# Division of a layer-1 attention stage among GpSimd, VectorE and DMA, and its order by half beats, in one fused two-layer kernel

## The chip, the core and the metric

One core of one Trainium2 chip. The metric is the device time of one launch in microseconds (us); lower is better. PE is TensorE's matmul, PEld its weight load, DVE is VectorE, ACT is ScalarE, POOL is GpSimd, SP is SyncE, which here only issues DMAs.

## The reference, cut to what matters

The whole program is two transformer-like layers over 2048 tokens (4 batches of 512) of 512 channels. The change touches only the last stage, layer 1:

```
xn = layernorm(x);  q = xn @ Wq.T                    # 32 heads of 16 channels
q, k = rmsnorm(q), rmsnorm(k)                        # per head
o  = softmax(q k^T / 4) v                            # keys and values of ctx_2048
x3 = x + tanh(g) * o
# spline layer, per token:
xf = layernorm(x3)*gamma + beta
tile = argmax over 64 tiles of sign scores (first the best of 8 clusters)
s  = the 8 channels of xf that belong to that tile
mn, mx = min and max of s over all tokens that chose the same tile
out = x3 + tanh(g2) * (xf, with those 8 channels replaced by a spline of (s-mn)/(mx-mn))
```

So attention needs the queries of a whole batch, and the very last result (the spline) needs the minimum and maximum over all tokens.

## The kernel before, in words

`phase_back` (from L1420) does this stage in one block, with one straight-line instruction list per engine. Time is counted in half beats `h` from -18 to 80. Each engine runs `for h in range(START, END)` and calls, in a written order, the steps whose slot plus lag equals `h`; each engine takes its list strictly in order and waits on semaphores. There are three kinds of work:

- **Groups of heads** (`g_at`): 32 groups, eight for each batch, group n from half beat 2n. PE computes scores (`scores`, L1643), ACT the exponentials (`exps`, L1818, 8 per group), PE multiplies by the values (`weigh`, L1655) into one of two PSUM tiles `atpO`. At lag 2 DVE copies that tile out (`evacuate`, L1862), PE transposes it (`turn`, L1662), and at lag 3 DVE divides by the sums (`normalise`, L1868 and L1869, into `o`). `weigh` of group n waits for `normalise` of group n-2, since both use the same PSUM tile.
- **Query tiles** (`q_at` with `q_slot`, `n_at` with `n_slot`): 16 tiles of 128 tokens. The first four (FIRST) come before group 0. Of each later tile: SP loads `x2a` and `x1` (`load`, L1555 and L1556, lag -2); POOL adds them (`combine`, L1716, lag 0); DVE takes mean and variance (`spread`, L1874, lag 1), POOL the root (`root`, L1721), DVE normalises and casts to f16 (`norm`, L1883 and L1887, lag 2), POOL subtracts for the low half (`low`, L1725, lag 2), SP turns the tile with a transposing DMA (`turn`, L1561, lag 3), PE projects it (`project`, L1678, twelve matmuls, six at the end of one group and six in the next), DVE copies the result (`projected`, L1892, lag 6), POOL squares it (`square`, L1730), DVE sums (`squares`, L1901), for each pair of tiles takes the root by Newton steps (`roots`, L1910 to L1915), scales (`scale`, L1923), POOL casts (`high`, L1735), DVE subtracts (`parts`, L1929), SP stores to `qst` (`store`, L1565), and SP reads queries back by a transposing DMA (`queries`, lag -3) for each group.
- **Spline tiles** (`c_at` with `c_slot`): 16 tiles of 128 tokens, when the groups of their batch are done. POOL adds `o` to `x2` (`residual`, L1740, lag 0); DVE `spread2` (L1948 to L1954, lag 1), POOL `roots` (L1744), DVE `scales` (L1959 to L1961, lag 2), POOL `y` (L1748), ACT `signs` (L1823), DVE `choose` (L1967 to L1975, lag 4), POOL `gathers` (two indirect DMAs, L1752 and L1755, lag 5), DVE `inner` (L1980 to L1992, lag 6). After the last `inner` come a short chain on PE and DVE and 16 indirect scatters on POOL (L1782).

In each half beat DVE's written order is: `projected`, `evacuate`, `inner`, `choose`, `normalise`, `scales`, `parts`, `scale`, `squares` with `roots`, `spread2`, `norm`, `spread`. POOL's is: `gathers`, `residual`, `combine`, `low`, `root`, `roots`, `high`, `square`, `y`. Slots before:

```python
q_slot = [-16, -15, -14, -13, -4, -2, 0, 2] + [16 * b + 6 + 4 * j for b in range(2) for j in range(4)]
c_slot = [16 * b + 19 + 4 * j for b in range(3) for j in range(4)] + [65, 66, 67, 68]
n_slot = {i: q_slot[i] + 7 for i in range(5, NT, 2)}
```

Of the kernel before, what the change touches and what calls it, by code (L numbers as in the profile page):

```python
# [15 lines left out]
P = 128  # L16
# [296 lines left out]
def part_pair(ap, first, step):  # L313

    return bass.AP(ap.tensor, ap.offset + first * HD, [list(ap.ap[0]), [4 * HD, NH], [step * HD, 2], [1, HD]])

# [1113 lines left out]
def phase_back(nc, S, sb, ps, a, R, K, out, wq):  # L1430
# [15 lines left out]
    with ExitStack() as mem:  # L1446
# [5 lines left out]
        xin = [sb(mem, f"quxin{i}", [P, D]) for i in range(4)]  # L1452
# [29 lines left out]
        key = [sb(mem, f"lakey{i}", [P, NTILE]) for i in range(2)]  # L1482
        top = [sb(mem, f"latop{i}", [P, 8]) for i in range(2)]
# [5 lines left out]
        lo, hi = sb(mem, "lalo", [P, 1]), sb(mem, "lahi", [P, 1])  # L1489
        oh = sb(mem, "laoh", [P, NT, NTILE])  # L1490
        pen = sb(mem, "lapen", [P, 2, NTILE])
# [30 lines left out]
        def n_at(h, lag):  # L1522


            out_ = [It(i // 2, i % 2) for i in range(FIRST) if q_slot[i] + 7 + lag == h]
            for i, at in n_slot.items():
                out_ += [It((i - 1 + j) // 2, j) for j in range(2) if at + lag + j == h]
            return out_
# [22 lines left out]
        def _(e):  # L1551
            def load(it):
                r = slice(it.n * P, (it.n + 1) * P)
                S.wait(e, "qux2", it.back(4))
                e.dma_start(x2[:, it.n, :], R["x2a"][r, :]).then_inc(S.sem(f"quxin{it.n % 4}"), 16)  # L1555
                e.dma_start(xin[it.n % 4][:, :], R["x1"][r, :]).then_inc(S.sem(f"quxin{it.n % 4}"), 16)  # L1556

            def turn(it):
                S.wait(e, "quxl", it)
                S.wait(e, "quproj", it.back(2))  # L1560
                S.moved(e.dma_start_transpose(xT[it.p][:, :, :], xhl[it.p][:, :]), "quxT", it)  # L1561

            def store(it):
                S.wait(e, "qulo", it)
# [21 lines left out]
            def store_x3(it):  # L1586
                S.wait(e, "lax3", it)
# [20 lines left out]
            for h in range(START, END):  # L1608
                for it in q_at(h, 3):
                    turn(it)  # L1610
                for it in n_at(h, 3):
                    store(it)
                for it in g_at(h, -3):
                    if it.n > 2:
                        keys(it)
                    queries(it)
# [96 lines left out]
        def _(e):  # L1713
            def combine(it):
                e.wait_ge(S.sem(f"quxin{it.n % 4}"), 32 * (it.n // 4 + 1))
                S.done(e.tensor_tensor(x2[:, it.n, :], x2[:, it.n, :], xin[it.n % 4][:, :], ALU.add), "qux2")  # L1716
# [6 lines left out]
            def low(it):  # L1723
                wait_early(e, "quxh", it)
                S.done(e.tensor_tensor(xhl[it.p][:, D:], xs[it.p][:, :], xhl[it.p][:, 0:D], ALU.subtract), "quxl")  # L1725

            def square(it):
                wait_early(e, "quraw", it)
                S.wait(e, "quss", it.back(2))
                S.done(e.tensor_tensor(sq[it.p][:, :], raw[it.n % 4][:, :], raw[it.n % 4][:, :], ALU.mult), "qusq")  # L1730
# [27 lines left out]
            for h in range(START, END):  # L1758
                for it in c_at(h, 5):
                    gathers(it)  # L1760
                for it in c_at(h, 0):
                    residual(it)
                for it in q_at(h, 0):
                    combine(it)
                for it in q_at(h, 2):
                    low(it)
                for it in q_at(h, 1):
                    root(it)
                for it in c_at(h, 1):
                    roots(it)  # L1770
# [3 lines left out]
                for it in q_at(h, 6, FIRST):  # L1774
                    square(it)
# [75 lines left out]
        def _(v):  # L1851
# [3 lines left out]
            def into(b, g):  # L1855
                x = o[:, :, :].rearrange("p (b t) (h c) -> p b t h c", b=BATCH, h=G)
# [7 lines left out]
            def normalise(it):  # L1864
# [4 lines left out]
                S.done(v.tensor_tensor(into(b, g), bass.AP(x.tensor, x.offset, [list(x.ap[0]), [P, 4], [32, 4], [1, HD]]),  # L1869
                                       bcast(rc[:, 0, 0:1], [(4, 4), (1, 4), (0, HD)]), ALU.mult), "ato")  # L1870

            def spread(it):
                S.wait(v, "qux2", it)
# [5 lines left out]
            def norm(it):  # L1879
                S.wait(v, "qurstd", it)  # L1880
                line(v.tensor_scalar(rs[it.p][:, :], rstd[it.p][:, :], SA, None, ALU.mult))
                S.wait(v, "quxl", it.back(2))
                S.done(v.tensor_scalar(xs[it.p][:, :], x2[:, it.n, :], mv[it.p][:, 0:1], rs[it.p][:, :], ALU.subtract, ALU.mult), "quxs")  # L1883
                if it.n >= FIRST:
                    S.wait(v, "quxs", it)
                    S.wait_moved(v, "quxT", it.back(2))
                    S.done(v.tensor_copy(xhl[it.p][:, 0:D], xs[it.p][:, :]), "quxh")  # L1887
# [6 lines left out]
            def squares(it):  # L1894
                if it.n < FIRST:
                    S.wait(v, "qusqA", it)
                else:
                    v.wait_ge(S.sem("qusq"), it.n - FIRST + 1)
                S.wait(v, "quqn", it.back(4))
# [17 lines left out]
            def scale(it):  # L1917
# [4 lines left out]
                S.wait(v, "qulo", it.back(2))  # L1922
# [4 lines left out]
            def parts(it):  # L1927
                wait_early(v, "quhi", it)
                S.done(v.tensor_tensor(part_pair(qp[it.p][:, :], 2, 1), twice(qn[it.p][:, :]),  # L1929
# [206 lines left out]
```

## Time and profile before

| | us |
|---|---|
| median of 3 runs | 1255.49 (1254.92 to 1257.19) |
| the profiled execution, its own time | 1258.56 |
| its span, first to last instruction | 1256.6 |
| PE busy in the span | 982.5 (78%) |
| DVE busy | 723.0 (58%) |
| ACT busy | 660.0 (53%) |
| POOL busy | 568.9 (45%) |
| mean granted TensorE clock, share of full speed | 0.916 |

Busy time is the sum over the whole span, which has stages with different limits; the stage of this change runs from about 800 us to the end, its groups from 852 to 1164 us. In a timeline row the columns are: start, duration, engine, line, operation, output and inputs, shapes, and in brackets the idle time just before it with what ended it. "DMA_TRANSPOSE" and "DMA_DIRECT2D" rows of SPq are issues.

### The profile page before, as it was taken

The numbers are of one execution on the slowest core, as the hardware profiler recorded it, in microseconds if no ns is written. First come the engines' busy times: TensorE is split into PE (matmuls) and PEld (weight loads), VectorE is DVE, ScalarE is ACT, GpSimd is POOL, SyncE is SP. The second block draws the span as 40 slices with busy tenths as digits, with TensorE's granted clock in tenths as the row PEclk, the third lists the DMA queues.
The fourth block names the chain that finished last, engine by engine and source line by source line (L and its number), as shares of the span: only waits on it lengthen the run. The fifth ranks groups of instructions, "written<-read, shape, count | busy, mean of one in ns | idle before, by whom it ended". The sixth has DMA issues, their size and how long they took to land. (4 is left out here: it accounts for less than half of the span.)

```text
span 1256.6 us, 27755 instructions
## 1 busy us (share of the span) xinstructions
PE 982.5 (78%) x9407; PEld 558.8 (44%) x9408; DVE 723.0 (58%) x1715; ACT 660.0 (53%) x1064; POOL 568.9 (45%) x483
## 2 busy tenths in 40 slices
PE   3689989868999696999999999238998778788000
PEld 1455656455676474777777777111222111111000
DVE  6676755489896374222232222254757886766875
ACT  3555645345543385444454444147888567799100
POOL 0232321266674364555565555423334444544635
PEclk9899999989999898999999999678999889899555
DMA  7343231599982887666766666575776565573110
GB/s 256 98 164 115 91 121 63 166 194 187 241 210 53 297 226 181 112 117 116 151 118 117 117 117 104 128 172 122 149 164 158 139 131 140 117 144 89 68 35 3
DMA packets 188066, 172.50 MB, mean 137 GB/s; under 512 B 141874, under 2 KB 143218, under 8 KB 187058
## 3 DMA queue, kind: packets, MB, share of 16 engines
q1 hardware_dynamic: 162096, 117.19, 36.0%
q0 software_dynamic: 24576, 53.83, 21.9%
q8 instruction: 59, 0.97, 0.3%
q10 hardware_dynamic: 1298, 0.20, 0.1%
q14 instruction: 37, 0.30, 0.1%
HBM read 81.12 MB, written 65.23 MB: 116 GB/s over the span
## 5 line engine op out<-in xcount | busy, mean ns | idle before, releaser
L1818 ACT ACTIVATE sb_atp<-ps_atpS 128x1024 f32<-128x1024 f32 x256 | 243.3, 1034 | 57.6 <-PE ps_atpS L1643 57.4
L1405 PEld LDWEIGHTS ps_shpH<-sb_roxT,sb_rowt 128*128 (+1 forms) x2844 | 167.3, 106 | 20.1 <-DVE sb_roxT L1272 1.9
L1405 PE MATMUL ps_shpH<-sb_roxT,sb_rowt 128*128 128x128 f16 (+1 forms) x2844 | 171.8, 219 | 1.7 <-DVE sb_roxT L1272 1.7
L1394 PE MATMUL ps_shpY<-sb_rowt,sb_rohhl 128*128 (+1 forms) x711 | 169.5, 384 | 3.8 <-DVE sb_rowt L1285 3.0
L1655 PE MATMUL ps_atpO<-sb_atp,sb_atv 128*17 128x512 f32 x1024 | 140.9, 623 | 35.8 <-ACT sb_atp L1818 19.1
L1029 POOL DMA_INDIRECT sb_roxg<-xn,sb_roentry x79 | 87.2, 1104 | 92.4 <-DMA sb_roentry<-list 72.9
L1128 ACT ACTIVATE sb_roh<-ps_shpH,sb_rob 128x128 f32<-128x128 f32 (+1 forms) x237 | 68.9, 362 | 101.4 <-PE ps_shpH L1405 98.9
L1394 PEld LDWEIGHTS ps_shpY<-sb_rowt,sb_rohhl 128*128 128x128 f16 (+1 forms) x711 | 67.4, 99 | 72.1 <-issue 8.6
L1643 PE MATMUL ps_atpS<-sb_atq,sb_atk 64*128 64x512 f16 x512 | 81.4, 398 | 20.3 <-DMA sb_atq<-qst 20.0
L1117 ACT ACTIVATE sb_roy<-ps_shpY,sb_roentry 128x512 f32<-128x512 f32 x79 | 54.2, 686 | 78.9 <-PE ps_shpY L1394 72.8
L1017 POOL DMA_INDIRECT list<-sb_shentry,sb_shposb x64 | 72.5, 1133 | 34.6 <-DVE sb_shposb L1200 19.7
L1036 POOL DMA_INDIRECT x<-sb_roy,sb_roentry x39 | 62.3, 1596 | 49.0 <-ACT sb_roy L1117 47.3
L1036 POOL DMA_INDIRECT x2a<-sb_roy,sb_roentry x40 | 64.9, 1622 | 40.1 <-ACT sb_roy L1117 37.7
L1272 DVE COPY sb_roxT<-ps_shpR 128x1024 f16<-128x1024 f16 x40 | 27.6, 690 | 92.4 <-PE ps_shpR L277 92.4
L1678 PE MATMUL ps_atpO<-sb_rowt,sb_quxT 128*128 128x512 f16 x192 | 50.5, 408 | 32.0 <-DMA sb_quxT<-sb_quxhl 27.0
L1272 DVE COPY sb_roxT<-ps_shpC 128x1024 f16<-128x1024 f16 x39 | 26.9, 690 | 80.7 <-PE ps_shpC L277 80.7
L1330 PEld LDWEIGHTS ps_shpH<-sb_shxT,sb_shw 128*128 128x128 f16 (+1 forms) x1152 | 68.3, 109 | 3.3
L1330 PE MATMUL ps_shpH<-sb_shxT,sb_shw 128*128 128x128 f16 (+1 forms) x1152 | 69.3, 223 | 0.0
L1277 DVE TENSOR_TENSOR sb_rohhl<-sb_roh,sb_rohhl 128x384 f16<-128x384 f32 x79 | 44.0, 557 | 43.4 <-ACT sb_rohhl L1133 43.3
L1340 PE MATMUL ps_shpY<-sb_shw,sb_shhh 128*128 128x512 f16 (+1 forms) x192 | 60.9, 400 | 5.1 <-DVE sb_shhl L1205 5.1
L1655 PEld LDWEIGHTS ps_atpO<-sb_atp,sb_atv 128*17 128x17 f32 x1024 | 17.6, 96 | 97.8 <-ACT sb_atp L1818 67.0
L1218 DVE SCALAR_TENSOR_TENSOR sb_rowt<-sb_rowt 128x1408 f16<-128x1408 f32 (+1 forms) x30 | 49.4, 1687 | 20.3 <-ACT sb_rowt L1085 20.3
(300 smaller groups left out, 1828.1 us busy)
## 6 DMA issues: line engine op xcount, KB each, us to landing
sb_rowt<-rw SPq DMA_DIRECT2D x15, 768.0 KB, 10.1
sb_rowt<-rw SPq DMA_DIRECT2D x15, 704.0 KB, 7.4
kst<-sb_kykp SPq DMA_DIRECT2D x16, 512.0 KB, 3.1
qst<-sb_quqp SPq DMA_DIRECT2D x16, 512.0 KB, 3.4
vst<-sb_kyvt SPq DMA_DIRECT2D x16, 272.0 KB
sb_atv<-vst SPq DMA_DIRECT2D x32, 136.0 KB, 3.4
sb_stage<-ctxT SPq DMA_DIRECT2D x4, 1024.0 KB, 7.0
sb_shxin<-x SPq DMA_DIRECT2D x16, 256.0 KB, 9.9
```

What stands on the lines that cost most here:

```text
L1017: S.moved(e.indirect_dma_start(out=R["list2"], out_offset=bass.IndirectOffsetOnAxis(ap=posb[it.p][:, k:k + 1], axis=0), in_=entry[:, it.n, ...
L1029: S.moved(e.indirect_dma_start(out=xg[it.p][:, :], out_offset=None, in_=R["xn2"], in_offset=bass.IndirectOffsetOnAxis(ap=rentry[:, n, 0:1] ...
L1036: S.moved(e.indirect_dma_start(out=R["x1" if it.p else "x2a"], out_offset=bass.IndirectOffsetOnAxis(ap=rentry[:, n - 5, 0:1], axis=0), in_ ...
L1128: last = e.activation(rh[0:n, f * P:(f + 1) * P], rpH[it.p][0:n, f * P:(f + 1) * P], ACT.Relu, bias=rb1[0:n, bass.ds(ex["bias"] * FB + f, ...
L1272: S.done(v.tensor_copy(rxT[it.p][:, :, :], rpT[it.p]), "roxT")
L1330: last = e.matmul(pH[it.p][s][0:n, f * P:(f + 1) * P], w[:, o:o + n], x[:, k, :], start=j == 0, stop=j == len(terms) - 1)
L1340: last = e.matmul(pY[it.p][:, :], x[0:n, s, k * P:(k + 1) * P], w[0:n, s * W2 + k * D:s * W2 + (k + 1) * D], start=j == 0, stop=j == len(t ...
L1394: last = e.matmul(pY[it.p][:, :], hhl[it.p][0:n, x, k * P:(k + 1) * P], weight(value, 2 * W1 + w + k * D, n, D), start=j == 0, stop=j == l ...
L1405: last = e.matmul(rpH[it.p][0:n, f * P:(f + 1) * P], weight(ex["up"], w + k * FF + f * P, P, n), rxT[it.p][:, x + k, :], start=j % (3 * KD ...
L1643: last = e.matmul(pS[n % 3][:, s * SEQ:(s + 1) * SEQ], k[at][r, j, m * P:(m + 1) * P], q[at][r, j, :], start=True, stop=True)
L1655: last = e.matmul(pO[it.p][32 * i:32 * i + n, :], vv[it.n % 3][:, m, i * n:(i + 1) * n], pr[(it.n * 8 + 2 * m + i // 2) % 6][:, (i % 2) * ...
L1818: S.done(e.activation(pr[n % 6][:, :], pS[n % 3][:, :], ACT.Exp, scale=HD ** -0.5 / SA ** 2), "atexp")
```

## The change

Slots, lags, owners and orders of this stage change; nothing before L1420 does.

- The sum of `x2a` and `x1` for tiles 4 to 15 is made by an accumulating DMA that POOL issues at lag -1 (`second`), on top of the plain load of `x2a`; tiles 4 to 7 are loaded at half beat -10, ahead of `keys`.
- For tiles 4 to 15 the f16 cast moves from DVE to POOL (`cast`), the low-half subtraction from POOL to DVE (`low`, lag 3), the square from POOL to DVE, and `parts` writes one part, which POOL copies to the other place (`again`).
- POOL's `residual` is gone; DVE's `normalise` adds each group's `o` to `x2` itself.
- `inner` keeps only a maximum (the minimum as the maximum of the negative), and comes at lag 7.
- Query tiles 8 to 15 come sooner, `c_slot` is 2 lower (1 lower for the last four), `queries` has lag -2, `turn` lag 4 for tiles 4 to 15, and the order in a half beat is new on DVE, POOL and SP.

```diff
-        q_slot = [-16, -15, -14, -13, -4, -2, 0, 2] + [16 * b + 6 + 4 * j for b in range(2) for j in range(4)]
-        c_slot = [16 * b + 19 + 4 * j for b in range(3) for j in range(4)] + [65, 66, 67, 68]
-        n_slot = {i: q_slot[i] + 7 for i in range(5, NT, 2)}
+        q_slot = [-16, -15, -14, -13, -4, -2, 0, 2, 6, 8, 12, 14, 20, 22, 30, 32]
+        c_slot = [16 * b + 17 + 4 * j for b in range(3) for j in range(4)] + [64, 65, 66, 67]
+        n_slot = {i: q_slot[i] + 8 for i in range(5, NT, 2)}
...
+                for it in g_at(h, -2):
+                    queries(it)
...
                 for it in q_at(h, -2):
-                    load(it)
+                    if it.n < FIRST or it.n >= 2 * FIRST:
+                        load(it)
...
                 if h == -10:
+                    for n in range(FIRST, 2 * FIRST):
+                        load(It(n // 2, n % 2))
...
+            def second(it):
+                e.wait_ge(S.sem(f"quxin{it.n}"), 16)
+                e.dma_start(x2[:, it.n, :], R["x1"][it.n * P:(it.n + 1) * P, :], accum_op=ALU.add).then_inc(S.sem(f"quxsum{it.n}"), 16)
...
+            def cast(it):
+                S.wait(e, "quxs", it)
+                S.wait_moved(e, "quxT", it.back(2))
+                S.done(e.tensor_copy(xhl[it.p][:, 0:D], xs[it.p][:, :]), "quxh")
...
-            def residual(it):
-                b = it.n // 4
-                e.wait_ge(S.sem("ato"), G * (b + 1))
-                S.done(e.tensor_tensor(x2[:, it.n, :], x2[:, it.n, :], o[:, it.n, :], ALU.add), "lax3")
+            def again(it):
+                S.reach(e, "qupl", it, it.n - FIRST + 1)
+                S.done(e.tensor_copy(one_part(qp[it.p][:, :], 3), one_part(qp[it.p][:, :], 2)), "qulo")
...
+                S.wait(v, "ato", it)
+                S.done(v.tensor_tensor(into(x2, b, g), into(x2, b, g), into(o, b, g), ALU.add), "lax3")
...
+            def low(it):
+                wait_early(v, "quxh", it)
+                S.done(v.tensor_tensor(xhl[it.p][:, D:], xs[it.p][:, :], xhl[it.p][:, 0:D], ALU.subtract), "quxl")
...
+                    line(v.tensor_tensor(sq[it.p][:, :], raw[it.n % 4][:, :], raw[it.n % 4][:, :], ALU.mult))
```

POOL's new order in a half beat: `combine` (tiles 0 to 3), `low` (tiles 0 to 3) or `cast`, `high`, `again`, `root`, `second`, `gathers`, `roots`, `y`. DVE's new order: `norm`, `scale`, `parts`, `spread`, `low`, `evacuate`, `projected`, `normalise`, `squares`, `roots`, `scales`, `choose`, `spread2`, `inner` (lag 7).

## Rows read from the trace of the kernel before

**Rows 1.** Windows: span; busy PE, PEld, DVE, ACT, POOL (instructions); clock; DMA share; GB/s.
```profile
912.00:947.08 35.08, 32.84 (x234) 7.69 (x234) 18.85 (x45) 30.37 (x32) 11.14 (x11) 1.00 0.76 174
947.08:1062.33 115.25, 90.99 (x582) 20.41 (x582) 90.19 (x233) 79.03 (x85) 54.46 (x47) 0.90 0.59 140
1062.33:1100.83 38.50, 29.66 (x210) 5.78 (x209) 29.47 (x87) 30.54 (x34) 18.12 (x13) 0.91 0.50 114
1100.83:1164.15 63.32, 54.44 (x412) 11.02 (x408) 38.15 (x137) 60.37 (x67) 27.25 (x20) 1.00 0.53 113
1164.15:1214.35 50.20, 0.66 (x4) 0.42 (x4) 41.48 (x155) 3.15 (x5) 30.30 (x24) 0.54 0.18 62
```

**Rows 2.** Waits, 865 to 1100.83 us: total us, times, longest.
```profile
PE ps_atpO L1655 <- DVE sb_o L1869: 12.6, 5, 5.2
...
PE ps_atpO L1662 <- DVE sb_atoT L1862: 6.0, 3, 2.7
PE ps_atpO L1678 <- DVE sb_o L1869: 5.1, 5, 2.0
```

**Rows 3.** Timeline of PE: two projection halves at different clock levels.
```profile
986.94 2.72 PE L1678 MATMUL ps_atpO<-sb_rowt,sb_quxT 128*128 128x512 f16 x6 [0.79 <-DVE sb_o L1869]
...
991.72 1.47 PE L1678 MATMUL ps_atpO<-sb_rowt,sb_quxT 128*128 128x512 f16 x6
```

**Rows 4.** Timeline, all engines, 971 to 979 us.
```profile
971.33 1.22 DVE L1981 TENSOR_SCALAR sb_lapen<-sb_lakey,sb_latop 128x64 f32<-128x64 f32 x1
...
973.13 1.10 DVE L1987 TENSOR_TENSOR sb_laxf<-sb_laxf,sb_latab 128x8 f32<-128x8 f32 x1
...
976.11 1.05 PE L1655 MATMUL ps_atpO<-sb_atp,sb_atv 128*17 128x512 f32 x8 [1.29 <-DVE sb_o L1869]
...
978.81 1.26 POOL L1716 TENSOR_TENSOR sb_x<-sb_x,sb_quxin 128x512 f32<-128x512 f32 x1
...
978.95 1.20 DVE L1913 TENSOR_TENSOR sb_qunt<-sb_qurr 128x64 f32<-128x64 f32 x1
```

**Rows 5.** Timeline of DVE beside POOL's scale and POOL's cast.
```profile
976.32 2.51 POOL L1748 TENSOR_SCALAR sb_o<-sb_x,sb_laab 128x512 f32<-128x512 f32 x1 [2.11 <-DVE sb_laab L1960]
...
978.17 0.23 DVE L1913 TENSOR_TENSOR sb_qunt<-sb_qurr 128x64 f32<-128x64 f32 x1
...
1075.15 1.04 POOL L1735 CAST sb_quqp<-sb_quqn 128x1024 f16<-128x1024 f32 x1 [3.05 <-DVE sb_quqn L1923]
...
1075.97 0.30 DVE L1970 SCALAR_TENSOR_TENSOR sb_lakey<-sb_lacs,sb_lats 128x64 f32<-128x64 f32 x1
```

**Rows 6.** Lines by form, 851 to 1165 us: count | busy us, mean ns | idle before.
```profile
L1929 DVE TENSOR_TENSOR sb_quqp<-sb_quqn,sb_quqp 128x1024 f16<-128x1024 f32 x12 | 14.6, 1216 | 0.5 <-POOL sb_quqp L1735 0.5
...
L1923 DVE TENSOR_TENSOR sb_quqn<-sb_quraw,sb_qurr 128x512 f32<-128x512 f32 x12 | 8.2, 682 | 0.0
...
L1887 DVE CAST sb_quxhl<-sb_quxs 128x512 f16<-128x512 f32 x11 | 4.7, 428 | 0.4
```

**Rows 7.** Timeline of DVE late in the spline tiles: where steps begin.
```profile
1190.27 0.21 DVE L1959 TENSOR_SCALAR sb_laab<-sb_lars,sb_gate 128x1 f32<-128x1 f32 x1
...
1193.16 0.69 DVE L1967 TENSOR_REDUCE sb_lats<-sb_lasg 128x64 f32<-128x512 f16 x1
...
1204.01 0.25 DVE L1980 TENSOR_SCALAR sb_laoh<-sb_lakey,sb_latop 128x64 f32<-128x64 f32 x1
...
1208.75 0.25 DVE L1980 TENSOR_SCALAR sb_laoh<-sb_lakey,sb_latop 128x64 f32<-128x64 f32 x1
```

**Rows 8.** Timeline of SP and PE at the start of the groups.
```profile
832.90 0.43 SPq L1555 DMA_DIRECT2D sb_x<-x2a  x1
...
851.83 1.46 PE L1643 MATMUL ps_atpS<-sb_atq,sb_atk 64*128 64x512 f16 x6 [20.03 <-DMA sb_atq<-qst]
```

**Rows 9.** DMA issues, whole span: KB each, median us to landing.
```profile
sb_rowt<-rw SPq DMA_DIRECT2D x15, 768.0 KB, 10.1
...
sb_x<-x2a SPq DMA_DIRECT2D x16, 256.0 KB, 3.6
```

More of the change, by code:

```diff
@@ L315, in part_pair, with one_part @@
     return bass.AP(ap.tensor, ap.offset + first * HD, [list(ap.ap[0]), [4 * HD, NH], [step * HD, 2], [1, HD]])
+def one_part(ap, at):
+    return bass.AP(ap.tensor, ap.offset + at * HD, [list(ap.ap[0]), [4 * HD, NH], [1, HD]])
 def twice(ap):
@@ L1526, in n_at @@
             for i, at in n_slot.items():
-                out_ += [It((i - 1 + j) // 2, j) for j in range(2) if at + lag + j == h]
+                out_ += [It((i - 1 + j) // 2, j) for j in range(2) if at + lag == h]
             return out_
@@ L1609, in _ @@
                 for it in q_at(h, 3):
+                    if it.n < FIRST:
+                        turn(it)
+                for it in q_at(h, 4, FIRST):
                     turn(it)
@@ L1615, in _ @@
                         keys(it)
-                    queries(it)
                 for it in c_at(h, 1):
@@ L1758, in _ @@
             for h in range(START, END):
[L1759 to L1762, printed above, removed]
                 for it in q_at(h, 0):
-                    combine(it)
+                    if it.n < FIRST:
+                        combine(it)
                 for it in q_at(h, 2):
[L1766 to L1770, printed above, removed]
+                    if it.n < FIRST:
+                        low(it)
+                    else:
+                        cast(it)
                 for it in n_at(h, 1):
@@ L1773, in _ @@
                         high(it)
-                for it in q_at(h, 6, FIRST):
-                    square(it)
+                for it in n_at(h, 2):
+                    if it.n >= FIRST:
+                        again(it)
+                for it in q_at(h, 1):
+                    root(it)
+                for it in q_at(h, -1, FIRST):
+                    second(it)
+                for it in c_at(h, 5):
+                    gathers(it)
+                for it in c_at(h, 1):
+                    roots(it)
                 for it in c_at(h, 2):
@@ L1894, in squares @@
             def squares(it):
+                S.wait(v, "quqn", it.back(4))
                 if it.n < FIRST:
@@ L1993, in inner @@
+                line.go(v.tensor_copy(xf[:, t, :], xb[:, 1, :]))
+                line(v.tensor_scalar(xb[:, 0, :], xb[:, 1, :], -1.0, None, ALU.mult))
+                line(v.tensor_reduce(top2[:, :], xb[:, :, :], AX.X, ALU.max))
+                line.go(v.scalar_tensor_tensor(run[:, 0, :], pen[:, :], top2[:, 0:1], run[:, 0, :], ALU.add, ALU.max))
+                S.done(v.scalar_tensor_tensor(run[:, 1, :], pen[:, :], top2[:, 1:2], run[:, 1, :], ALU.add, ALU.max), "larun")
                 S.wait(v, "larun", it)
@@ L1995, in _ @@
             for h in range(START, END):
+                for it in q_at(h, 2):
+                    norm(it)
+                for it in n_at(h, 1):
+                    scale(it)
+                for it in n_at(h, 2):
+                    parts(it)
+                for it in q_at(h, 1):
+                    spread(it)
+                for it in q_at(h, 3, FIRST):
+                    low(it)
+                for it in g_at(h, 2):
+                    evacuate(it)
                 for it in q_at(h, 6, FIRST):
@@ L1997, in _ @@
                     projected(it)
-                for it in g_at(h, 2):
-                    evacuate(it)
-                for it in c_at(h, 6):
-                    inner(it)
+                for it in g_at(h, 3):
+                    normalise(it)
+                for it in q_at(h, 7):
+                    squares(it)
+                for i, at in n_slot.items():
+                    if at == h:
+                        roots(i)
+                for it in c_at(h, 2):
+                    scales(it)
@@ L2002, in _ @@
                 for it in c_at(h, 4):
                     choose(it)
-                for it in g_at(h, 3):
-                    normalise(it)
-                for it in c_at(h, 2):
-                    scales(it)
-                for it in n_at(h, 2):
-                    parts(it)
-                for it in n_at(h, 1):
-                    scale(it)
-                for i, at in n_slot.items():
-                    if at == h:
-                        squares(It(i // 2, i % 2))
-                        roots(i)
@@ L2016, in _ @@
-                for it in q_at(h, 7):
-                    if it.n not in n_slot:
-                        squares(it)
                 for it in c_at(h, 1):
                     spread2(it)
-                for it in q_at(h, 2):
-                    norm(it)
-                for it in q_at(h, 1):
-                    spread(it)
+                for it in c_at(h, 7):
+                    inner(it)
                 if h == -14:
```

92 lines of the change are left out of this document (42 added, 50 removed).

## The prediction

> **What bounds the kernel now.** I read the page first (no engine is busy through the span), then windows cut at events of this stage [rows 1]. The cuts are starts of DVE's copies: up to 1062.33 us those of projected tiles, after that those of finished groups. From 912.00 to 947.08 there are four groups and two projected tiles, no spline work: 17.54 us for a pair of groups with one tile. From 1100.83 to 1164.15 there are eight plain groups: 63.32 / 8 = 7.92 us each, ACT busy 60.37 of 63.32. These two are the pace that PE and ACT set by themselves; a projected tile costs 17.54 - 2 x 7.92 = 1.7 us. In between both tiles and spline work run: 947.08 to 1062.33 is ten groups with five tiles in 115.25 us where that pace would give 5 x 17.54 = 87.7, so 27.5 us are lost; 1062.33 to 1100.83 is four groups in 38.50 against 31.7, so 6.8 more. **34.3 us** of stalls in all. Before 947 us I count none that this change can reach.
>
> The waits say who is late [rows 2]: PE stood 12.6 + 6.0 + 5.1 = 23.7 us for DVE's `normalise` and `evacuate`. Much of the rest is clock: after such a stall the granted clock is at its lower level (1.2 instead of 2.4 GHz) for a few us, and a projection half takes 2.72 instead of 1.47 us [rows 3]; the window's mean clock is 0.90 against 1.00 on both sides [rows 1]. DVE is not merely idle behind a long chain: it is busy 90.19 of 115.25 us with 233 instructions, and `normalise` stands in its list behind `inner` or `choose`. The timeline shows why that is long: DVE instructions of about 0.2 us take 1.1 to 1.2 us while POOL adds two tensors [rows 4]. The same line L1913 takes 1.20 us beside POOL's sum [rows 4] and 0.23 us beside POOL's scale [rows 5].
>
> The last two windows are serial: 50.20 us from the last `evacuate` to the last `inner`, then 42.25 us (1256.60 - 1214.35) of spline end and scatters.
>
> **The change, part by part.**
>
> *DVE's load in the crowded stretch.* Take 90.19 busy us, plus a gap of some 0.035 us behind each of 233 instructions (8; estimated from the starts in the timeline), as occupied: 98 us in ten groups. About three stretched instructions per pair of groups (as between 971 and 979 us, rows 4), at 1.2 - 0.23 = 0.97 us, make 14.5 us, an estimate; without them 83.8. The moves add: per query tile a square 0.68 and a low half 0.68 (priced by L1923's 0.682), less the cast 0.43 and less 1.22 - 0.68 = 0.54 of `parts` [rows 6], net +0.4; per group the added sum, half of L1923's elements, about 0.4. Ten groups, five tiles: 83.8 + 2 + 4 = 90 us, or 9.0 per group. But tiles 8 to 11 project at groups 5, 6, 8, 9 now and the rest at 12, 13, 17, 18, so that the crowded stretch, groups 9 to 21, holds 4.5 tiles in 13 groups: I get 109 us for DVE where PE and ACT want 13 x 7.92 + 4.5 x 1.7 = 110.6. DVE thus fits, barely.
>
> *The order.* `evacuate` and `normalise` now precede all spline work of their half beat, and `projected` no longer stands before `evacuate`. By half beats the work between `evacuate` and `normalise` is mostly 4 to 5 us; it is 8.0 us at group 10 (`roots` 3.0, `spread2` 2.0, `scale` and `spread`, `low`), 7.3 at group 14 and 6.4 at group 19. From `evacuate` to the `weigh` that needs `normalise` is one period, 7.9 us, less 1.2 for the two steps. So three places stall PE or, through a late `signs` in ACT's list, the exponentials: some 1 to 2 us each, and the clock after them.
>
> *POOL's casts.* Whether they hold DVE up is weakly shown: L1970 takes 0.30 us at the end of a cast, against about 0.23 [rows 5]. POOL casts more now: per tile 1.04, plus two of half that size. Bounds for the eight late tiles: 0 (as beside POOL's scale) to 8 x 2.1 = 17 us if DVE were held through each. I take 4 us of DVE time, nearer the scale's row, since half of DVE's instructions have one tensor input. Together I leave 8 us of the 34.3: **-26**. Ends: -34 and -15.
>
> The Trainium skill's page "SBUF — State Buffer", section "Who interferes with whom", says that a DVE instruction with two SBUF inputs contends with any GpSimd instruction that reads SBUF, and that the later of the two is blocked until the first has finished. The casts would then block like the sums, and by it the term would be about -19 instead of -26; but it would have blocked L1913 beside POOL's 2.51 us scale as well, and there the trace disagrees (0.23 us, rows 5).
>
> *The end.* Tile 11's `spread2` and `scales` are now done before the last group. After the last `evacuate` (0) PE's turn and `normalise` with its sum end at about 5.9 us, with `inner` of tile 10 beneath. Then DVE has `choose` x 5, `spread2` x 4, `scales` x 4, `inner` x 5. `scales` with `spread2` takes 1193.16 - 1190.27 = 2.9 us, `inner` with `choose` 1208.75 - 1204.01 = 4.7 [rows 7]: 4 x 2.9 + 5 x 4.7 = 35.1, to 41.0. POOL, freed of four sums of 1.27 us, is followed step by step at 0.7 us for a root, 2.1 for `y`, 2.4 for two gathers: it delays DVE by some tenths, and each gather has landed before its `inner`, seven half beats behind. 41.5 against 50.20: **-8.7**. One more dependent step in `inner` costs 0.1 x 5: **-8.2**. Ends -3 (POOL late again) and -11. The end after `inner` is unchanged: one reduction of double size replaces two.
>
> *The start.* PE's first scores wait 20.03 us for queries [rows 8], at the end of a chain of stores through SP. Four loads now issue before `keys`, at about 0.5 us each: +2; the pair of loads before the sign rows goes, -1.3. Net **+0.7**, ends -1 and +3 (1 MB more traffic in front of `keys`). POOL's accumulating DMA has no row with this form. Bounds: it lands like a plain load, 3.6 us, or like the slowest loads, 10.1 us [rows 9]. It is issued two half beats (8 us) before `spread` asks; I take 5 us, nearer the load of its size: 0. If it is later, `spread`, `low` and `evacuate` behind it on DVE wait. In the first two late tiles `root` stands before `second` on POOL, so `spread` of tile 5 waits, which `project` at the end of group 1 still covers. Issuing it takes POOL about as long as the sum it replaces. SP has fewer issues; `queries` one half beat later still leaves 8 us.
>
> **Sum**: -26 - 8.2 + 0.7 = -33.5. The profiled execution took 1258.56 us (span 1256.6 and 2.0 around it): 1225.0. The median of the runs shown is 3.1 lower: **1222.0 us**.
>
> **Rivals.**
> 1. *DVE becomes the bound.* 109 against 110.6 us leaves nothing for unevenness; casts block and `signs` comes late. For it: the numbers above; ACT, too, takes its list in order. Then the crowded stretch gives back only half, -13: 1235.
> 2. *The pace is reached.* All 34 us go, since lag is absorbed over several groups: 1222 - 8 = 1214, with the better end of the tail 1212.
> 3. *The change doesn't do what it says:* stalls move to other groups, only the end gains: about 1247. Against it: the order puts the urgent steps first.
> 4. *Slower: the accumulating DMA lands late.* Place: DVE's wait at `spread`, before `evacuate` and `normalise`, for 12 tiles. Up to 8 us it is hidden; each us beyond costs 12. The gain is used up at 33.5 / 12 = 2.8, so from a landing of 10.8 us on the kernel is slower; at 12 us it takes 1222 + 48 = 1270. For it: 768 KB loads took 10.1 us, the write needs a read of the target, and DMA share is already 0.59 to 0.76. Against it: 3.6 us for this size.
>
> **How the numbers follow.** The forecast has 0.46 (own range 1216 to 1228), rival 1 0.22, rival 2 0.18, rival 3 0.06, rival 4 0.08. The range takes in the forecast, rivals 1 and 2 and the ends of the start: 1209 to 1240. About 0.2% (2.5 us) is what a measurement of this kernel can tell from no change; the runs shown spread over 2.3. Faster than that: 0.91 (the forecast and rivals 1 to 3, less a hundredth that falls near the bound), within it 0.01, slower 0.08 (rival 4).
>
> **What would show it.** In the new profile: the projection pairs and groups between 947 and 1100 us come 8 to 9.5 us apart; PE's waits for `sb_o` and `sb_atoT` fall from 23.7 to under 8 us, the clock there rises from 0.90; two-input DVE lines lose their 1.1 to 1.2 us members; from the last `evacuate` to the last `inner` 40 to 43 us; first scores within 3 us of 851.8. Wrong if DVE waits for the summing DMA, if L1913-like lines stay stretched beside casts, or if PE waits for `sb_o` as long as before.

## The result, and the profile after

| | before | after |
|---|---|---|
| median of 4 runs each, us | 1256.17 (1254.92 to 1257.19) | 1237.76 (1236.31 to 1242.23) |
| ratio, 95% interval | | 0.986 (0.9833 to 0.9887) |
| profiled execution, its own time / span | 1258.56 / 1256.6 | 1236.31 / 1234.5 |
| first scores to first `evacuate` | 13.25 | 11.16 |
| **groups**: first to last `evacuate` (31 intervals) | 299.07 | 286.47 |
| last `evacuate` to last `inner` | 50.16 | 41.86 |
| from there to the end | 42.26 | 43.17 |

The kernel is 18.4 us faster by the medians, 22.3 by the two profiled executions, where 33.5 was forecast. 1237.8 lies in the range of 1209 to 1240, near rival 1 (1235), but outside the forecast's own range of 1216 to 1228. The windows of the changed kernel, cut at starts of `evacuate` for groups 0, 9, 21, 31 and at the end of the last `inner` (span; busy PE, PEld, DVE, ACT, POOL; clock; DMA share; GB/s):

```profile
863.00:951.25 88.25, 80.72 (x553) 19.94 (x552) 63.41 (x153) 69.11 (x73) 26.78 (x29) 1.00 0.80 161
951.25:1070.78 119.53, 101.39 (x682) 22.39 (x680) 97.35 (x295) 94.42 (x103) 52.64 (x48) 0.93 0.69 144
1070.78:1149.47 78.69, 67.74 (x514) 13.82 (x512) 51.17 (x181) 75.84 (x85) 27.68 (x21) 1.00 0.63 120
1149.47:1191.33 41.86, 0.66 (x4) 0.42 (x4) 36.52 (x147) 2.52 (x4) 23.68 (x19) 0.56 0.22 74
```

The same cuts before gave 82.61, 133.08, 83.38 and 50.16 us. So the first nine groups became 5.6 us longer, the middle twelve 13.5 shorter, the last ten 4.7 shorter, the end 8.3 shorter. Of the 5.6, 3.0 come with the new slots (85.23 in e6, which has the old ones): one more query tile now falls in these groups. The other 2.6 are there with the old slots too, and are gone when `roots` is split (82.61 in e11, as before). Of the query tiles, 9 to 13 and 15 come sooner; 8 and 14 keep their half beats 6 and 30. The clock in the middle is 0.93 against 0.90 in [rows 1], and 1.00 on both sides again. PE's waits from 863 to 1100 us (total, times, longest), against [rows 2]:

```profile
PE ps_atpO L1668 <- ACT sb_atp L1839: 13.5, 38, 1.2
PE ps_atpO L1668 <- DVE sb_o L1890: 5.8, 2, 3.9
PE ps_atpO L1668 <- DVE sb_quraw L1918: 4.3, 12, 0.6
PE ps_atpO L1691 <- DVE sb_o L1890: 3.8, 4, 1.2
PE ps_atpO L1675 <- DVE sb_atoT L1883: 2.1, 2, 1.4
```

The waits for `sb_o` and `sb_atoT` fell from 23.7 to 11.7 us, not below 8. Where they sit is seen in the timeline of DVE around group 10, the worst place, which answers to [rows 4]:

```profile
958.23 0.68 DVE L1926 TENSOR_TENSOR sb_qusq<-sb_quraw 128x512 f32<-128x512 f32 x1
...
959.76 0.68 DVE L1997 TENSOR_REDUCE sb_lats<-sb_lasg 128x64 f32<-128x512 f16 x1
...
962.74 0.68 DVE L1883 COPY sb_atoT<-ps_atpO 128x512 f32<-128x512 f32 x1
963.34 0.21 DVE L1937 TENSOR_SCALAR sb_qunt<-sb_quss 128x64 int32<-128x64 int32 x1
...
966.16 0.69 DVE L1978 BATCH_NORM_STATS2 sb_last<-sb_x 128x6 f32<-128x512 f32 x1
...
968.14 1.29 DVE L1950 TENSOR_TENSOR sb_quqn<-sb_quraw,sb_qurr 128x512 f32<-128x512 f32 x2
969.35 0.69 DVE L1900 BATCH_NORM_STATS2 sb_qust<-sb_x 128x6 f32<-128x512 f32 x1
...
970.36 1.50 DVE L1913 TENSOR_TENSOR sb_quxhl<-sb_quxs,sb_quxhl 128x512 f16<-128x512 f32 x1
971.78 0.24 DVE L1889 RECIPROCAL sb_atrc<-ps_atpO 128x16 f32<-128x16 f32 x1
...
974.69 1.28 DVE L1960 TENSOR_TENSOR sb_quqp<-sb_quqn,sb_quqp 128x512 f16<-128x512 f32 x2
975.90 0.68 DVE L1883 COPY sb_atoT<-ps_atpO 128x512 f32<-128x512 f32 x1
```

DVE does not pause once from 958.2 to 976.5. `squares` and `choose` (L1926 to L2005) and a `norm` stand before `evacuate` at 962.74; then `roots`, `spread2`, two `scale`, `spread` and `low` before `normalise` at 971.78. The other engines at that moment:

```profile
968.90 2.42 POOL L1752 CAST sb_quqp<-sb_quqn 128x1024 f16<-128x1024 f32 x2 [0.19 <-DVE sb_quqn L1950]
...
973.30 2.51 POOL L1764 TENSOR_SCALAR sb_o<-sb_x,sb_laab 128x512 f32<-128x512 f32 x1 [1.04 <-DVE sb_laab L1990]
```
```profile
972.63 1.05 PE L1668 MATMUL ps_atpO<-sb_atp,sb_atv 128*17 128x512 f32 x8 [3.93 <-DVE sb_o L1890]
...
975.49 1.91 PE L1668 MATMUL ps_atpO<-sb_atp,sb_atv 128*17 128x512 f32 x8 [0.83 <-ACT sb_atp L1839]
```
```profile
973.89 0.63 ACT L1844 ACTIVATE sb_lasg<-sb_law 128x512 f16<-128x512 f32 x1 [4.09 <-DVE sb_law L1991]
```

PE stood 3.93 us, and then runs at the lower of its clock's two levels (1.2 instead of 2.4 GHz; 1.91 instead of 1.05 us for eight matmuls) for the next few us; ACT stood 4.09 us in front of `signs`, which waits for DVE's `scales`.

What the lower clock cost here can be read from a second execution of the same kernel, run `e9`. It had 6.8 us at the lower level in groups 0 to 31, where the one above had 17.1, and its middle stretch took the same time (to be held against 119.53 us, busy PE 101.39 and clock 0.93 above):

```profile
962.91:1082.46 119.55, 98.27 (x682) 21.67 (x680) 97.34 (x294) 94.41 (x103) 52.67 (x48) 0.97 0.70 144
```

PE was busy 3.1 us less and nothing ended sooner. In these groups PE's slower matmuls fell into time in which it would have waited for DVE.

For what follows I cost DVE's steps from the starts of instructions in the timeline: norm 0.65, scale 0.6, parts 0.6, spread 1.0, low 0.65, evacuate 0.6, projected 0.6, normalise 1.1, squares 1.5, roots 2.8, scales 0.9, choose 2.3, spread2 2.0, inner 2.3 us. A plain group leaves 7.92 / 2 = 3.96 us for each half beat. The intervals of groups 0 and 1 hold one projected tile each and take 9.88 us, so a tile costs 9.88 - 7.92 = 1.96 us, where I had 1.7.

### The profile page after: what moved, and what is told of

Read it like the earlier page. It is cut to its first block and busy times, and to the rows that moved or that the text cites. A ratio compares the mean times of both kernels' runs of the same rounds, so it can differ in the third digit from the quotient of the medians.

```text
span 1234.5 us, 27760 instructions
## 1 busy us (share of the span) xinstructions
PE 981.3 (79%) x9407; PEld 561.6 (45%) x9408; DVE 718.4 (58%) x1757; ACT 659.3 (53%) x1064; POOL 538.6 (44%) x467
## 3 DMA queue, kind: packets, MB, share of 16 engines
q0 software_dynamic: 26304, 56.98, 24.1%
## 5 line engine op out<-in xcount | busy, mean ns | idle before, releaser
L1410 PEld LDWEIGHTS ps_shpH<-sb_roxT,sb_rowt 128*128 (+1 forms) x2844 | 170.1, 107 | 21.1 <-DVE sb_roxT L1277 1.8
L1410 PE MATMUL ps_shpH<-sb_roxT,sb_rowt 128*128 128x128 f16 (+1 forms) x2844 | 174.4, 221 | 1.7 <-DVE sb_roxT L1277 1.7
L1399 PE MATMUL ps_shpY<-sb_rowt,sb_rohhl 128*128 (+1 forms) x711 | 172.1, 388 | 2.5 <-DVE sb_rowt L1290 2.1
L1041 POOL DMA_INDIRECT x2a<-sb_roy,sb_roentry x40 | 65.1, 1627 | 41.5 <-ACT sb_roy L1122 39.4
L1282 DVE TENSOR_TENSOR sb_rohhl<-sb_roh,sb_rohhl 128x384 f16<-128x384 f32 x79 | 44.0, 557 | 43.2 <-ACT sb_rohhl L1138 42.9
L1656 PEld LDWEIGHTS ps_atpS<-sb_atq,sb_atk 64*128 64x128 f16 x512 | 14.8, 95 | 102.8 <-ACT sb_atp L1839 44.8
```

Source lines behind the costliest of these rows:

```text
L1041: S.moved(e.indirect_dma_start(out=R["x1" if it.p else "x2a"], out_offset=bass.IndirectOffsetOnAxis(ap=rentry[:, n - 5, 0:1], axis=0), in_ ...
L1399: last = e.matmul(pY[it.p][:, :], hhl[it.p][0:n, x, k * P:(k + 1) * P], weight(value, 2 * W1 + w + k * D, n, D), start=j == 0, stop=j == l ...
L1410: last = e.matmul(rpH[it.p][0:n, f * P:(f + 1) * P], weight(ex["up"], w + k * FF + f * P, P, n), rxT[it.p][:, x + k, :], start=j % (3 * KD ...
L1656: last = e.matmul(pS[n % 3][:, s * SEQ:(s + 1) * SEQ], k[at][r, j, m * P:(m + 1) * P], q[at][r, j, :], start=True, stop=True)
```

## The experiments

The parts of the program ahead of this stage vary by chip and run: first scores came at 851.84 us in the profiled execution above and at 863.48 in that of `e9`, the same kernel. The stage itself is far steadier: its groups took 286.47 and 286.51 us, its end 41.86 and 41.90. It is not always that steady. e6 and e10 give every engine the same work up to group 21, and their groups 9 to 21 took 118.73 and 119.62 us; from first scores to the first `evacuate` runs with the same lists up to there took 11.16 us (changed, e9, e10) or 11.83 to 12.11 (e4, e6, e7, e8). Each segment comes from one profiled execution. So I compare segments of the stage and read nothing into differences of less than 1 us, while a ratio is good to about 0.4%. "Stage" is first scores to the end of the last `inner`.

| run | ratio (95%) | groups | of it 0-9 / 9-21 / 21-31 | end | stage |
|---|---|---|---|---|---|
| before | 1 | 299.07 | 82.61 / 133.08 / 83.38 | 50.16 | 362.5 |
| changed | 0.986 | 286.47 | 88.25 / 119.53 / 78.69 | 41.86 | 339.5 |
| e1 order undone | 0.9855 (0.9815-0.9894) | 286.43 | 84.59 / 124.03 / 77.81 | 42.25 | 342.5 |
| e2 sums on POOL | 0.9856 (0.9815-0.9897) | 284.31 | 86.32 / 119.29 / 78.70 | 44.41 | 340.3 |
| e3 urgent first | 0.9871 (0.9833-0.9909) | 290.29 | 89.07 / 122.14 / 79.08 | 41.84 | 344.2 |
| e4 one Newton step | 0.9789 (0.9750-0.9828) | 278.55 | 84.48 / 114.90 / 79.17 | 42.10 | 332.8 |
| e5 order and owners undone | 0.9957 (0.9936-0.9978) | 294.73 | 86.09 / 129.62 / 79.02 | 45.53 | 353.4 |
| e6 all slots undone | 0.9808 (0.9780-0.9835) | 280.39 | 85.23 / 118.73 / 76.43 | 46.08 | 338.5 |
| e7 query slots undone | 0.9895 (0.9872-0.9918) | 295.12 | 88.77 / 125.01 / 81.34 | 41.84 | 348.8 |
| e8 spline slots undone | 0.9863 (0.9834-0.9893) | 285.53 | 88.24 / 118.33 / 78.96 | 46.06 | 343.4 |
| e9 changed again | 0.9831 (0.9797-0.9865) | 286.51 | 88.26 / 119.56 / 78.69 | 41.90 | 339.6 |
| e10 old slots, early end | 0.9773 (0.9737-0.9809) | 281.21 | 85.22 / 119.62 / 76.37 | 41.85 | 334.2 |
| e11 and roots split | 0.9765 (0.9722-0.9807) | 278.11 | 82.61 / 119.12 / 76.38 | 41.84 | 331.1 |
| e12 and pairs apart | 0.9756 (0.9715-0.9798) | 280.75 | 82.26 / 120.23 / 78.26 | 41.88 | 334.6 |

**e1, order undone.** DVE's loop calls `projected`, `evacuate`, `inner`, `choose`, `normalise`, `scales`, `parts`, `scale`, `squares`, `roots`, `spread2`, `low`, `norm`, `spread`.

> The changed kernel with one part undone: DVE calls its steps in the order of before within a half beat (projected, evacuate, inner, choose, normalise, scales, parts, scale, squares, roots, spread2, low, norm, spread); owners, slots and lags stay as changed. Against 1237.8 us of the changed kernel and 31 groups in 286.5 us from first to last evacuate. Theory A (the order is what gained, because evacuate and normalise no longer stand behind spline work): the 31 groups take 294 to 300 us again and the kernel 1246 to 1252. Theory B (the gain is the sums taken from POOL, which stretched DVE's instructions by 19.8 us before and 4.4 now): 286 to 289 us and 1237 to 1241, since the order only shifts who is late.

286.43 us: theory A falls, B's number holds. But within the groups it is not the same run: the middle is 4.5 us longer, the rest 4.5 shorter, and the first `evacuate` is again 2.7 us later (13.84 after the first scores), since it stands behind `projected`. So the stage is 3.0 us longer.

**e2, sums on POOL.** The square leaves DVE's `squares`, `low` DVE's loop and the added sum `normalise`; POOL does them, `low` behind `cast`.

```diff
                     else:
                         cast(it)
+                        low(it)
+                for it in q_at(h, 6, FIRST):
+                    square(it)
...
+                for it in c_at(h, 0):
+                    residual(it)
...
-                S.wait(v, "ato", it)
-                S.done(v.tensor_tensor(into(x2, b, g), into(x2, b, g), into(o, b, g), ALU.add), "lax3")
...
-                    line(v.tensor_tensor(sq[it.p][:, :], raw[it.n % 4][:, :], raw[it.n % 4][:, :], ALU.mult))
...
-                for it in q_at(h, 3, FIRST):
-                    low(it)
```

> The changed kernel with another part undone: the low half, the square and the residual are sums of POOL again (the cast stays on POOL too, and the sum of the two loads stays an accumulating DMA); order and slots stay as changed. Theory B: DVE instructions of 0.2 and 0.7 us stretch to 1.2 again, the 31 groups take 294 to 300 us, the end 45 us, the kernel 1249 to 1255. Theory A: the stretched instructions now lie behind the urgent steps, so the groups take 286 to 290 us, and only the end is longer by the four sums, 1240 to 1245.

284.31 us, shorter than either theory allowed: B falls too. The stretched instructions are back (DVE's and POOL's timeline of this run):

```profile
985.47 1.23 POOL L1742 TENSOR_TENSOR sb_quxhl<-sb_quxs,sb_quxhl 128x512 f16<-128x512 f32 x1
985.60 1.15 DVE L2023 TENSOR_SCALAR sb_lapen<-sb_lakey,sb_latop 128x64 f32<-128x64 f32 x1
```

Adding up, for each DVE instruction of the groups, what it takes beyond the lower quartile of its line and shape: 22.0 us before, 7.6 changed, 22.1 here. But DVE has 12 squares, 12 low halves and 32 sums less to do, 24 x 0.68 + 32 x 0.43 = 30 us. Giving POOL's sums to DVE trades some 14.5 us of being held up for 30 of own work. Only the end needed it: 44.41 against 41.86.

**e3, urgent first.** `evacuate` and `normalise` are called first in each half beat.

> The changed kernel with evacuate and normalise as the very first steps of each half beat on DVE, ahead of norm, scale, parts, spread and low too; nothing else is moved. Theory C (what is left is lateness: at groups 10, 14 and 18 about 8 us of DVE work lie between evacuate and normalise; the new order cuts this to 5.7 at most, since the query steps of the next half beat no longer come before normalise): PE's 11.7 us of waits for sb_o and sb_atoT fall below 5, the intervals of 13.2, 13.9 and 10.9 us fall to about 10, the 31 groups take 274 to 280 us, the kernel 1226 to 1232. Theory D (DVE has simply too much work in groups 9 to 20, in whatever order): the waits move to other steps, 284 to 288 us, 1235 to 1239. Slower, 1240 or more, if what feeds SP (parts, norm) comes late and the queries with it.

290.29 us, worse than either theory; by the groups it is nearest to D. PE's waits for `sb_o` fell as C said, but the lateness came back through ACT, which takes `signs` in order, and through `sb_quraw`. PE's waits in the same stretch as above (877 to 1117 us of this run) and ACT's longest:

```profile
PE ps_atpO L1668 <- ACT sb_atp L1839: 21.3, 38, 4.9
PE ps_atpO L1668 <- DVE sb_quraw L1918: 7.4, 11, 3.1
PE ps_atpO L1668 <- DVE sb_o L1890: 1.7, 1, 1.7
```
```profile
990.42 0.63 ACT L1844 ACTIVATE sb_lasg<-sb_law 128x512 f16<-128x512 f32 x1 [5.47 <-DVE sb_law L1991]
```

The ratio, 0.9871 of 1256.2 us or 1240.0, would fit the third case of the expectation, but not its reason: PE waited for queries only once, at the start.

**e4, one Newton step.** `for _ in range(3)` of `roots` becomes `range(1)`: two of the three refinements of the root are left out.

> The changed kernel with one Newton step instead of three in roots (two thirds of that refinement are left out of the computation, so the roots are coarser): 6 small instructions, about 1.6 us of DVE time, less in each of six half beats, 4 of them from group 7 on. Theory C or D, DVE late or full: each of the four places in the crowded stretch gives back more than the 1.6 us, since the fall of the clock after the wait goes too: the 31 groups take 276 to 281 us, the kernel 1228 to 1233. Theory E (the stalls come from blocked instructions beside POOL's casts or from PE's own clock, not from DVE's amount of work): 285 to 287 us, 1236 to 1238.

278.55 us, as theories C and D had it; E falls. Six `roots` lose 6 x 0.26 = 1.56 us each, 9.4 in all, and the groups give back 7.9: 3.8 in the first nine (three of them), 4.6 in the middle (the other three, 4.7 us of DVE). In the middle DVE's time is worth what it takes; the further gain by the clock that I had put into the expectation is not there.

**e5, order and owners undone.** The edits of e1 and e2 together, and the cast back in DVE's `norm`.

> The changed kernel with both undone at once: DVE's order of before, and the low half, the square, the residual on POOL and the cast on DVE as before; the new slots, the lags and the accumulating DMA stay. Undone singly, neither lengthened the 31 groups (286.4 us without the order, 284.3 with the sums on POOL, 286.5 as changed, 299.1 before). Theory F (the slots did it, order and owners are a wash): 283 to 290 us again, and the end 45 us. Theory G (either of the two is enough, since a stretched instruction harms only where an urgent step stands behind it, and the order harms only where instructions are stretched): 295 to 302 us, and the kernel within 3 us of before.

294.73 us: between F and G, at G's edge. Undone singly, the two parts cost 0 and -2.2 us in the groups; together with the cast they cost 8.3. That suggests that they stand in for each other, but the run has a third difference: the cast gives DVE 12 x 0.43 = 5.2 us of work more, and was not moved alone. How much of the 8.3 is its share is open. POOL's `residual` and the rest also lengthen the end by 3.7.

**e6, all slots undone.** The lines `q_slot` and `c_slot` as before; `n_slot` stays at +8.

> The changed kernel with the slots of query tiles and spline tiles as before (one query tile in two groups up to group 19, c_slot 2 later, 1 later for the last four); order and owners stay as changed. Theory F: the 31 groups take 296 to 302 us, the end 44 to 47 us, since tile 11 of the spline work lies behind the last group again. Theory G: 285 to 290 us, only the end is longer.

280.39 us, better than both theories and 6.1 **better** than the change. The middle stretch:

```profile
954.66:1073.39 118.73, 101.92 (x714) 23.02 (x712) 97.13 (x300) 97.62 (x107) 53.81 (x47) 0.99 0.79 154
```

The end is 4.2 us longer, so the new slots pay 4.2 there and cost 6.1 in the groups. The clock of 0.99 is no explanation: e2 has it too, with 284.31 us.

**e7, query slots undone**, and **e8, spline slots undone**: one of the two lines each.

> Only the slots of the query tiles as before, c_slot as changed. Theory F with the query tiles as the cause (6.5 of them ran beside spline work before, 4.5 now): 295 to 301 us for the 31 groups, the end unchanged at 42 us. If the spline slots were the cause: 285 to 290 us. Theory G: 285 to 290 us.

> Only c_slot as before (2 later, 1 later for the last four), query tiles as changed. Theory F with the query tiles as the cause: the 31 groups 284 to 289 us, since the spline work only shifts by a group, and the end 44 to 47 us: 1240 to 1243 against 1237.8 on a chip where before takes 1256. If the spline slots carry part of the gain in the groups: 290 us or more.

295.12 and 285.53 us. Taken alone, e7 looks like theory F; with e6 beside it F is false. Old query slots are good with old spline slots and bad with new ones: what counts is how the two fall on the same half beats. DVE's work, from the step costs above, for the two half beats in which group n is evacuated and normalised, and the interval to the next `evacuate`:

| group | 9 | 10 | 11 | 12 | 13 | 14 | 15 |
|---|---|---|---|---|---|---|---|
| changed: work / interval | 7.1 / 11.5 | 10.9 / 13.2 | 8.8 / 8.1 | 6.7 / 9.8 | 8.4 / 10.9 | 9.6 / 13.9 | 9.8 / 8.8 |
| e6 | 9.2 / 8.9 | 5.0 / 9.1 | 8.0 / 9.0 | 11.3 / 13.8 | 9.2 / 8.5 | 7.3 / 9.1 | 8.0 / 9.0 |
| e7 | 8.6 / 10.9 | 5.6 / 7.5 | 9.7 / 10.8 | 9.6 / 14.1 | 10.9 / 10.8 | 5.6 / 7.5 | 9.7 / 10.8 |

e7 has e6's work, only with the spline steps two half beats sooner. In e6, `squares` is followed by `scales` (0.9) before the next `evacuate`; in e7 by `choose` (2.3). The chain shows it (DVE in e6, then in e7; in brackets the idle time before):

```profile
961.10 0.68 DVE L1926 TENSOR_TENSOR sb_qusq<-sb_quraw 128x512 f32<-128x512 f32 x1
...
962.63 0.21 DVE L1989 TENSOR_SCALAR sb_laab<-sb_lars,sb_gate 128x1 f32<-128x1 f32 x1
...
963.54 0.69 DVE L1883 COPY sb_atoT<-ps_atpO 128x512 f32<-128x512 f32 x1
...
968.17 0.26 DVE L1889 RECIPROCAL sb_atrc<-ps_atpO 128x16 f32<-128x16 f32 x1 [2.94 <-PE ps_atpO L1675]
```
```profile
962.02 0.68 DVE L1926 TENSOR_TENSOR sb_qusq<-sb_quraw 128x512 f32<-128x512 f32 x1
...
963.56 0.68 DVE L1997 TENSOR_REDUCE sb_lats<-sb_lasg 128x64 f32<-128x512 f16 x1
...
965.90 0.69 DVE L1883 COPY sb_atoT<-ps_atpO 128x512 f32<-128x512 f32 x1
...
969.49 0.25 DVE L1889 RECIPROCAL sb_atrc<-ps_atpO 128x16 f32<-128x16 f32 x1
```

e6 has 2.94 us to spare, e7 none. Intervals of 10.8 to 11.0 us occur again and again where `squares` and `choose` share a half beat: in the changed kernel (groups 13, 17; 11.5 at group 9), in e7 and in e8. That this pair is the cause was read from the traces, not tried alone.

**e9, the changed kernel again.**

> The changed kernel itself once more, on the chip of the next three, to see how much of a segment is noise. All theories: 31 groups in 285 to 288 us (286.5 before), 41.9 us to the end of the last inner, 0.984 to 0.989 of the kernel before.

As expected in the segments, to 0.05 us; its ratio of 0.9831 lies just below the 0.984 expected, with an interval that overlaps.

**e10, old slots, early end.**

```diff
-        c_slot = [16 * b + 17 + 4 * j for b in range(3) for j in range(4)] + [64, 65, 66, 67]
+        c_slot = [16 * b + 19 + 4 * j for b in range(2) for j in range(4)] + [49, 53, 57, 61, 64, 65, 66, 67]
```

> The run with all slots undone, but with the spline slots of the third and fourth batch early as in the change (49, 53, 57, 61, then 64 to 67). Query tiles and the first eight spline tiles keep the slots of before. Theory H (the new query and spline slots overlap on DVE: the half beats 21 to 24 and 29 to 33 want 5 to 6.4 us each where a half beat of PE is 4; the old slots have at most three such in a row, so the groups are better off with them, and only the end needs the early slots): 31 groups in 279 to 283 us, 42 us to the last inner, and 0.975 to 0.979 of before. If the 280.4 us of the run with all slots undone were luck: 284 to 288 us and 0.981 or more.

281.21 and 41.85 us, 0.9773: theory H holds. Query tiles end before the third batch's spline work, so early slots cost nothing there.

**e11, roots split.** `roots` does its first Newton step one half beat earlier (`at - 1 == h`), the other two at `at`.

> The kernel of the run before, and roots split: its first Newton step one half beat earlier, behind squares, the other two where all three were. DVE does the same instructions. Theory H (unevenness: half beats 26, 34 and 42 hold 3.0 us of roots and 2.6 of inner at once): the three intervals of about 13.7, 13.6 and 11.6 us lose some 1.2 each, 31 groups 2 to 4 us shorter than the run before. Theory D (only the amount of DVE work counts): the same within 1 us.

3.1 us shorter as a whole, as H said, but not where H said. In the middle the three heavy intervals lost 1.4, 1.2 and 1.2 us (13.8, 13.6, 11.6 to 12.4, 12.4, 10.3) and those before them gained as much (9.0, 8.8, 9.0 to 10.3 each): 119.62 to 119.12, no difference that counts, which is D's answer. The gain, 2.6 us, is in the first nine groups, where the half beat before had room.

**e12, pairs apart.** `n_at` shifts the second tile of a pair by a half beat (`at + lag + j == h`), and the last query tile comes at 32 instead of 34; so two things differ from e11.

> The kernel of the run before, and the two tiles of a pair are scaled, cast and stored one half beat apart, as in the kernel before the change (last two query tiles at 30 and 32, so that their stores are not late). The same DVE work. Theory H: each of the heavy half beats loses another 0.7 us, 31 groups 1 to 3 us shorter than the run before. Theory D: the same within 1 us. Against both: 285 us or more if the later half of the pair makes the queries of a batch late, seen as a wait of PE for sb_atq.

A miss for both: 2.6 us longer than e11. 1.5 us is a second wait of PE for `sb_atq` (24.1 us in two waits, the longest 22.6, the start); for the rest, intervals of 12.9 and 12.3 us at groups 15 and 18, the cause stays open. By the ratio the last three cannot be told apart; by the stage e11 is the shortest. All three are faster than before. Against the changed kernel run beside them they are 5.0 to 8.5 us shorter in the stage; the ratios are 0.6 to 0.8% lower, but their intervals still overlap that of e9, so that in the whole time this is not shown.

## Why the prediction was right and wrong

**Start, not told from noise.** First scores came 50.37 us after the first load instead of 49.65, which is the +0.7 of the forecast. But `e9`, the same kernel, took 51.19, and e4, e6 to e8 and e10 to e12, with the same lists up to there, 50.5 to 53.0: one execution of each kernel does not show a term of 0.7 us. The agreement is luck. The accumulating DMA lands after 5.3 us (4.1 to 6.1; 5 taken; row of the DMA issues below), and POOL's issue of it takes 0.91 us. DVE waited 1.8 us for it in two waits in all the groups, and 7.9 us in two waits ahead of them (up to 4.7), where I had no wait. With no landing near the 10.8 us that rival 4 needs, it falls.

```profile
sb_x<-x POOLq DMA_DIRECT2D x12, 256.0 KB, 5.3
```

**End, right.** -8.3 against -8.2: 41.86 us, where 41.5 and 0.5 for the extra steps was forecast. The parts are now measured: early slots 4.2 (e6, e8), POOL without the sums 2.6 (e2) to 3.7 (e5, with the old order). What I did not have is +0.9 behind the last `inner`, the same in the changed kernel and in all twelve runs (43.2); up to the issue of the last scatter both kernels take 37.0 us, so it lies behind that, and is not explained.

**Groups, mis-sized.** -26 was forecast; -12.6 was measured, and another -2.1 before the first `evacuate`, which no longer waits for `projected` (with the old order, e1, it is 13.84 us again). Counted beyond the pace of 7.92 us for a group and 1.96 for a tile, groups 9 to 22 lost 31.5 us before and 15.2 now, and the first nine lose 3.7 more than before. So of the 13.4 us that are missing from the -26, 9.7 are missing in the crowded stretch and 3.7 went ahead of it.

The amount of DVE work was right: from 951.25 to 1070.78 us DVE was occupied all but 17.2 us (its waits), 102.3 for twelve groups, where 109 for thirteen makes 100.6. PE's pace for them is 12 x 7.92 + 4.5 x 1.96 = 103.9. The step that failed is the next one, "DVE thus fits, barely", and with it "three places stall ... some 1 to 2 us each". Two engines that want 102 and 104 us, and hand each other PSUM tiles in every half beat, took 119.5: each is idle while the other is late. I had compared one gap between `evacuate` and `normalise` with one period. But the heavy half beats come in runs: at groups 9 to 11 the three intervals are 32.8 us, where the pace with one tile is 25.7, at 14 to 16 they are 29.8 against 24.7 with half a tile: 7.1 and 5.1 us, not 1 to 2. The third place, groups 19 and 20, costs 1.1 as forecast, and group 13 costs 2.0, which I had not. "Before 947 us I count none" missed another: the interval of group 2 takes 11.94 against 9.88. It comes with the new order and not with the slots: 9.9 in e1, 11.9 with the old query slots (e6, e7), 10.6 with `roots` split. The term for the clock after a stall was at least too high for the changed kernel, where 10 us more or less at the lower level made no difference.

**The parts, in a wrong order of worth.** I took the stretched instructions for the main loss. They were as large as estimated (18.7 us in the twelve groups 9 to 20 before, 4.8 now; I had 14.5 in ten), but e2 shows that their removal is paid for by DVE's new work. I took the sooner query tiles for a relief of the crowded stretch; e6 shows that the slots cost 6.1 us in the groups. What gained is everything else together: e6 against before, -18.7 us. That neither the order nor the owners is needed by itself is shown (e1, e2); that both and the cast together are worth 8.3 us too (e5). But e5 is still 4.3 us shorter than before although it has the new slots. So the parts that no run undid, the accumulating DMA, the one-part `parts` and the lags of `queries`, `turn` and `inner`, may carry some of the gain; that was not tried.

**POOL's casts, right in size.** 3.9 to 5.4 us of the 7.6 stand beside a cast or the copy of `again`; 4 was taken. (The two figures differ by one `parts` of 2.19 us that overlaps a scale, a cast and a copy.) But they do block: `low` began at 970.36, just behind the second of the two casts (970.28 to 971.31), took 1.50 instead of 0.68 us and ended 0.5 us after that cast. There the Trainium skill, "SBUF — State Buffer", "Who interferes with whom", which holds that the later of the two is blocked until the first has finished, agrees with the trace. Beside POOL's scale it does not: from 974.69 two `parts`, each with two inputs in SBUF, took 0.68 us each under the scale that runs from 973.30 to 975.81. The term stays small because few two-input instructions meet a cast: three of twelve `low` did. The -19 that the prediction gave for the page's rule has no working there; with its own bound of 17 us for held casts the term would have been -26 + 17 - 4 = -13. 1.2 to 2.7 us of the stretch stand beside POOL's scale, which [rows 5] had shown as harmless.

**Rivals.** Rival 1 (half of it given back, 1235) came nearest in number (its -13 against -12.6, though that is -16.3 in the crowded stretch and +3.7 ahead of it) and in its reason, lack of evenness and late `signs`. That 1237.8 is in the range is owed to this rival, not to the forecast. Rival 2, that lag is absorbed over several groups, is the opposite of what the heavy runs show. The signs that I had named: waits under 8 us (11.7), groups 8 to 9.5 us apart (up to 13.9) and no stretch beside casts all failed; the end held, and first scores came within 3 us of 851.8 in the first execution.

## What to carry to other kernels

When two in-order engines that hand buffers to each other both come out near the stage's pace, do not take the larger sum as the time: list the work of each slot of the schedule and add it up over runs of neighbouring slots, for a run that is over its time is paid in full, and moving a step to its neighbour only moves the stall (e11 in the middle). The phase between two periodic kinds of work can be worth as much as the change itself: the same instructions took 280.4 or 295.1 us (e6, e7). Undo parts singly and together, since two parts that can stand in for each other each look worthless alone (e1, e2), and keep such a joint run free of a third part, which e5 is not.

## What the runs showed of the hardware

Not expected: the segments of this stage repeat to 0.05 us between two executions of the changed kernel, while the start of the stage moved by 11.6 us; between e6 and e10, though, a stretch with the same work differed by 0.9 us. The clock's lower level cost nothing where PE had to wait for DVE anyway: 17.1 and 6.8 us of it in the groups, 286.47 and 286.51 us for them. And a POOL cast and a two-input DVE instruction hold each other up, the later one being held. The cast at 968.90, begun while the second `scale` ran on DVE, took 1.43 us, where 1.04 is what one takes alone in [rows 5]. The next cast took 1.03, and `low`, begun just after it, 1.50 instead of 0.68.
